# Graph-attention kernel: first block's attention applied to relu(LN(x)) before the product with W0, with a new order on every engine

## What is computed

```python
def _L0_gnn_ref(h, adj, W, a):                      # first block
    Wh = jnp.einsum('bnf,fo->bno', h, W)
    e_src = Wh @ a1;  e_dst = Wh @ a2               # a1, a2: halves of a
    e = e_src[:, :, None] + e_dst[:, None, :]
    e = jnp.where(e > 0, e, 0.2 * e)
    e = jnp.where(adj > 0, e, NEG_INF)
    attention = jax.nn.softmax(e, axis=2)
    kth = jax.lax.top_k(attention, 16)[0][:, :, -1:]
    attention = jnp.where(attention < kth, 0.0, attention)
    return jax.nn.elu(jnp.einsum('bij,bjo->bio', attention, Wh))
def _L1_gnn_ref(x, adj, ...):                       # second block
    for l in range(3):
        # scores from x @ attn_w[l], masked softmax, agg = attn @ x
        h = layernorm(x + agg, g1[l], beta1[l])
        ff = gelu(h @ W1[l] + b1[l]) @ W2[l] + b2[l]
        x = layernorm(h + ff, g2[l], beta2[l])
h = jnp.maximum(_layernorm(x), 0.0);  x = x + _L0_gnn_ref(h, adj, W, a)
h = jnp.maximum(_layernorm(x), 0.0);  x = x + _L1_gnn_ref(h, adj, ...)
```

## Time and profile before

| | |
|---|---|
| median of 3 runs | 2964.74 us |
| the profiled execution's own time | 2969.18 us |
| its span, first to last instruction | 2967.5 us |
| TensorE matmul busy | 2822.2 us (95%) |
| ScalarE busy | 2460.3 us (83%) |
| GpSimd busy | 2229.7 us (75%) |
| VectorE busy | 2056.3 us (69%) |
| DMA engines, mean share | 12% in the middle of the run |

### The profile page before, as it was taken

How to read it: one execution, slowest core, us unless ns; L and a number is a source line. 1 busy time by engine, 2 the same in 40 slices (tenths; PEclk the granted TensorE clock), 3 DMA queues, 4 the chain that set the end, 5 groups by cost and what they waited for, 6 DMA issues and landing times.

```text
span 2967.5 us, 59504 instructions
## 1 busy us (share of the span) xinstructions
PE 2822.2 (95%) x17632; PEld 2510.8 (85%) x17632; DVE 2056.3 (69%) x7275; ACT 2460.3 (83%) x4887; POOL 2229.7 (75%) x2410
## 2 busy tenths in 40 slices
PE   4789999999999999999999999999999999999985
PEld 3678888888888888888889888888888888988874
DVE  4667777767777676867777777776777767776432
ACT  3578899888898888889988888988888888888763
POOL 0356878878787788777878877777878778888874
PEclk6789999999999999999999999999999999999997
DMA  5100010111101111111011110011110101110001
GB/s 154 36 26 26 26 33 17 34 26 32 34 26 21 30 33 25 33 28 32 18 33 25 33 33 27 17 33 34 24 34 26 34 17 33 24 33 19 10 10 15
DMA packets 96388, 89.38 MB, mean 30 GB/s; under 512 B 9120, under 2 KB 94368, under 8 KB 96032
## 3 DMA queue, kind: packets, MB, share of 16 engines
q1 hardware_dynamic: 79136, 68.32, 7.6%
q0 software_dynamic: 16896, 16.78, 4.3%
HBM read 47.34 MB, written 37.75 MB: 29 GB/s over the span
## 4 chain that ended last, share of the span: by engine, by line
PE 54%; POOL 13%; issue 11%; DVE 11%; DMA 2%; ACT 1%; POOLq 0%; DVEq 0%; ACTq 0%
PE ps_ff L1114 7%; PE ps_ff L1115 7%; PE ps_ff L1116 7%; PE ps_mm L1093 7%; PE ps_mm L1094 7%; PE ps_mm L1095 7%; POOL a_lo L417 3%; PE ps_ag L1151 3%; PE ps L1204 2%; DVE junk L930 2%; PE ps_ht L1165 2%; POOL H L424 2%; DMA out<-H 2%; POOL H L407 2%; POOL H L396 2%
## 5 line engine op out<-in xcount | busy, mean ns | idle before, releaser
L417 POOL TENSOR_TENSOR a_lo<-A,a_hi 128x512 fp32r<-128x512 f32 x576 | 759.9, 1330 | 433.6 <-ACT a_hi L540 423.0
L1114 PE MATMUL ps_ff<-w_hi,a_hi 128*128 128x256 f32 x3072 | 902.3, 294 | 19.3 <-issue 10.4
L1115 PE MATMUL ps_ff<-w_lo,a_hi 128*128 128x256 f32 x3072 | 864.9, 282 | 1.0 <-issue 0.7
L1116 PE MATMUL ps_ff<-w_hi,a_lo 128*128 128x256 f32 x3072 | 859.6, 280 | 0.0
L532 ACT ACTIVATE A<-ps_mm,b_col 128x512 f32<-128x512 f32 x768 | 524.2, 685 | 226.8 <-PE ps_ff L1116 138.8
L1093 PE MATMUL ps_mm<-ht_hi,w_hi 128*128 128x512 f32 x1536 | 655.0, 426 | 3.6 <-DVE ht_lo L981 2.8
L1114 PEld LDWEIGHTS ps_ff<-w_hi,a_hi 128*128 128x128 f32 x3072 | 578.2, 188 | 50.6 <-issue 30.5
L1094 PE MATMUL ps_mm<-ht_hi,w_lo 128*128 128x512 f32 x1536 | 608.0, 396 | 0.0
L1095 PE MATMUL ps_mm<-ht_lo,w_hi 128*128 128x512 f32 x1536 | 607.1, 395 | 0.0
L1115 PEld LDWEIGHTS ps_ff<-w_lo,a_hi 128*128 128x128 f32 x3072 | 578.9, 188 | 18.6 <-issue 3.9
L1116 PEld LDWEIGHTS ps_ff<-w_hi,a_lo 128*128 128x128 f32 x3072 | 579.2, 189 | 0.0
(11 more groups left out here) (111 smaller groups left out, 5186.5 us busy)
## 6 DMA issues: line engine op xcount, KB each, us to landing
xr<-in_x SPq DMA_DIRECT2D x32, 512.0 KB, 3.8
out<-x SPq DMA_DIRECT2D x32, 512.0 KB, 3.5
out<-H POOLq DMA_DIRECT2D x32, 512.0 KB, 6.0
mask_in<-mask_park SPq DMA_DIRECT2D x96, 128.0 KB, 3.0
adj_sb<-in_adj SPq DMA_DIRECT2D x32, 256.0 KB, 4.4
mask_park<-mask_out SPq DMA_DIRECT2D x32, 128.0 KB, 1.7
X<-in_L_gnn_W SPq DMA_DIRECT2D x3, 1024.0 KB, 5.1
H<-in_L_gnn_W SPq DMA_DIRECT2D x3, 1024.0 KB, 7.7
```

Source lines behind the costliest of these rows:

```text
L417: pool.tensor_tensor(a_lo[:, at], A[:, at], a_hi[:, at].bitcast(F32), ALU.subtract).then_inc(s["a_lo_gpsimd"], 1)
L1114: pe.matmul(out_g, a_hi[:, at, cols], w2_hi[:, l, m], start=first, stop=False, skip_group_check=True)
L1115: pe.matmul(out_g, a_hi[:, at, cols], w2_lo[:, l, m], start=False, stop=False, skip_group_check=True)
L1116: last = pe.matmul(out_g, a_lo[:, at, cols], w2_hi[:, l, m], start=False, stop=final, skip_group_check=True)
```

## The change

First block: `x0_norm` applies relu itself. The score vectors come from relu(LN(x)) in SBUF and the vectors W0 a1 and W0 a2, made once (`wa_sums`, `turn_wa`, `wa_copy`). `z_mix` applies the attention to relu(LN(x)), `mix_copy` brings that product to SBUF, and `z_agg` multiplies it with W0. `turn_h0`, `h0_copy`, `wh`, `wh_copy` and `wh_scores` are gone. The split of the eight low parts (two on VectorE, six on GpSimd) is as before. All five orders are new, the iteration begins at another place of the work, and the hardware loop has 22 iterations (4 to 25) in 11 trips; 18 are unrolled.

```diff
-FIRST, LAST = -4, NG + 3
-FIRST_STEADY, LAST_STEADY = 4, NG - 5
+FIRST, LAST = -5, NG + 3
+FIRST_STEADY, LAST_STEADY = 4, NG - 7
...
-                norm("x", k, lambda g: hn0[:, g], lambda g: xr[:, g], ACT.Identity, s["x_norm"])
+                norm("x", k, lambda g: hn0[:, g], lambda g: xr[:, g], ACT.Relu, s["x_norm"])
...
+            def mix_copy(k, half):
...
+                act.wait_ge(s["z_mixed"], value(n + 1))
                 if some(n):
+                    act.wait_ge(s["z_agg"], value(n))
+                act.activation(flat(mixed[:]), ps_0[:], ACT.Copy).then_inc(s["mix_copied"], 1)
...
+            def wa_sums():
+                dve.wait_ge(s["w0_in"], 16)
+                dve.wait_ge(s["a0_in"], 16)
+                for j in range(2):
+                    for c in range(DC):
+                        last = dve.tensor_tensor_reduce(
+                            out=junk[:, 2 * j + c], in0=w0[:, c], in1=a0_row[:, j], scale=1.0, scalar=0.0,
+                            op0=ALU.mult, op1=ALU.add, accum_out=wa_col[:, j, c:c + 1])
...
+            def e0_scores(k):
...
+                dve.wait_ge(s["x_norm"], value(k + 1))
...
+                for g in range(G):
                     for j in range(2):
                         last = dve.tensor_tensor_reduce(
+                            out=junk[:, 2 * g + j], in0=hn0[:, g], in1=wa_row[:, j], scale=1.0, scalar=0.0,
+                            op0=ALU.mult, op1=ALU.add, accum_out=e0[:, j, g:g + 1])
...
             def turn_e0(k):
-                pe.wait_ge(s["wh_copied"], value(k * 2 + 2))
+                pe.wait_ge(s["e0_made"], value(k + 1))
                 pe.wait_ge(s["mask_made"], value(k * 2 + 1))
+                if some(k):
+                    pe.wait_ge(s["z_out_made"], value(k * 2))
...
+            def z_mix(k, half):
...
+                pe.wait_ge(s["pt0_made"], value(k + 1))
+                if some(n):
+                    pe.wait_ge(s["z_out_made"], value(n))
+                for c in range(DC):
+                    for g in range(2):
+                        j = 2 * half + g
+                        last = pe.matmul(ps_0[:, (2 * c + g) * P:(2 * c + g + 1) * P], hn0[:, j, c * P:(c + 1) * P], pt0[:, j * P:(j + 1) * P],
+                                         start=(c == 0 and g == 0), stop=(c == DC - 1 and g == 1), skip_group_check=True)
...
             def z_agg(k, half):
-                pe.wait_ge(s["pt0_made"], value(k + 1))
...
-                    last = pe.matmul(ps_0[:, g * D:(g + 1) * D], pt0[:, j * P:(j + 1) * P], wh_sb[:, j],
-                                     start=(g == 0), stop=(g == 1), skip_group_check=True)
+                pe.wait_ge(s["mix_copied"], value(k * 2 + half + 1))
                 for g in range(2):
+                    for c in range(DC):
+                        last = pe.matmul(ps_0[:, g * D:(g + 1) * D], mixed[:, c, g * P:(g + 1) * P], w0[:, c],
+                                         start=(g == 0 and c == 0), stop=(g == 1 and c == DC - 1), skip_group_check=True)
...
+                masks(i + 2)
                 a_low(i, 0, 7)
-                masks(i + 2)
...
```

More of the change, by code:

```diff
@@ L452, in iteration @@
             def iteration(i):
[L453 to L479, removed]
@@ L1166, in turn_h @@
                 last.then_inc(s["h_turned"], 1)
-            def turn_h0(k, half):
-                if not here(k):
-                    return
-                n = k * 2 + half
-                pe.wait_ge(s["x_norm"], value(k + 1))
-                if some(n):
-                    pe.wait_ge(s["wh_copied"], value(n))
-                if some(k):
-                    pe.wait_ge(s["z_out_made"], value(k * 2))
-                for d in range(DC):
-                    for g in range(2):
-                        last = pe.transpose(ps_0[:, (2 * d + g) * P:(2 * d + g + 1) * P],
-                                            hn0[:, 2 * half + g, d * P:(d + 1) * P], ident[:])
-                last.then_inc(s["h0_turned"], 1)
             def w1_bias(l):
@@ L1192, in w1_bias, with turn_wa @@
                 last.then_inc(s["w1_biased"], 1)
[L1194 to L1206 removed]
+            def turn_wa():
+                pe.wait_ge(s["wa_summed"], 1)
+                for j in range(2):
+                    for c in range(DC):
+                        last = pe.transpose(ps_0[:, j * D + c * P:j * D + (c + 1) * P], wa_col[:, j, c:c + 1].to_broadcast([P, P]), ident[:])
+                last.then_inc(s["wa_turned"], 1)
             def turn_e0(k):
@@ L1247, in iteration @@
-                mm1(i - 1, 1, 3)
-                turn_p(i + 1, 0)
-                turn_h0(i + 2, 1)
-                mm1(i - 1, 1, 4)
-                agg(i + 1, 0, 0)
-                wh(i + 2, 1)
-                mm2(i - 1, 1, 0)
-                mm2(i - 1, 1, 1)
-                agg(i + 1, 0, 1)
-                turn_h(i - 2, 2, 0)
+                turn_h(i - 2, 2, 1)
+                turn_e0(i + 2)
                 mm2(i - 1, 1, 2)
                 mm1(i - 1, 1, 5)
-                turn_e0(i + 2)
+                agg(i + 1, 0, 1)
@@ L1271, in iteration @@
-                mm2(i - 1, 1, 7)
+                mm1(i - 2, 2, 2)
+                mm1(i - 2, 2, 3)
                 if peeled(i, -1):
                     w1_bias(2)
-                mm1(i - 2, 2, 2)
-                mm1(i - 2, 2, 3)
-                turn_h(i + 1, 0, 0)
                 mm2(i - 2, 2, 0)
-                turn_sj(i, 1)
                 mm1(i - 2, 2, 4)
```

413 lines of the change are left out of this document (214 added, 199 removed).

## The result

| | before | after |
|---|---|---|
| median of the runs, us | 2964.49 (2963.42 to 2964.8) | 2911.3 (2908.08 to 2913.98) |
| ratio | | 0.982, 95% interval 0.980 to 0.984 |
| profiled execution, us | 2969.2, span 2967.5 | 2913.98, span 2912.3 |

The changed kernel is faster by 53 us, the forecast was 28. The time lies in the range, between the forecast (2937) and rival B (2905). The views of the trace of after are read in the order of the prediction.

What follows compares the result with a forecast made beforehand. TensorE bounds the kernel: 85.7 us of work in an unrolled iteration of 85.92. Less work 27, waits in the loop 3, unrolled iterations minus 2, start and end zero: 28 off 2964.7 gives 2937 us, range 2904 to 2962, chance 0.55.

Steps and rivals of the forecast that it cites:

- rival B: The new order leaves only TensorE's wait at its branch, 32 us more gained: 2905 us, chance 0.14.
- TensorE's work: Removed and added matmuls and transposes: 6.04 us a group becomes 5.20, a gain of 0.85, 27 us in all.
- ScalarE: Two copies and two table loads fewer an iteration; the copy between `z_mix` and `z_agg` is covered; nothing counted.
- Place (a): `node_scores` of layer 0 no longer stands behind VectorE's branch, so the 1.33 us lost at `turn_sj` each trip goes.
- Place (c): `a_low` of chunk 7, now behind `y1_sum`, `y1_moments` and `masks`: about 1.3 us of VectorE's branch comes through once a trip.
- Place (b): First `mm2` of layer 0, waiting for `y_sum`: 0.5 to 0.6 us an iteration left as is, bounds 0 and 1.
- The sum of waits: About 4 us a trip in 11 trips, 44 against 47: a gain of 3; unrolled iterations a loss of 2.
- Start and end: Earlier first reductions against `x_moments` waiting for W0 and a: zero, between a gain of 8 and a loss of 8 us.
- C: Rival: VectorE's dense stretch ahead of layer 0's `y_sum` adds 0.5 us in some 30 iterations: 2952 us, chance 0.12.
- D: Rival, no change: a ring through ScalarE and VectorE sets the period, TensorE reaches the same waits earlier: about 2963, chance 0.06.
- E: Rival: masks slowed by GpSimd ahead of `a_low` of chunk 7, 1.9 us more in 31 iterations: 2996 us, chance 0.10.
- F: Rival of a dearer `z_mix`, outside the range of 2904 to 2962 us; size not in the text; chance 0.03.

Runs made afterwards that it cites:

- unshift_after: The changed kernel with `wa_col`, a tile of 16 bytes, moved to the end of the allocation, so tiles between stand where they stood before: 2952.0 us, ratio 0.995.
- pad64_before: The kernel before with an unused tile of 64 bytes a partition behind `a0_row`: 2971.9 us, ratio 1.002.
- pad64_after: The changed kernel with an unused tile of 64 bytes behind `wa_col`: 2956.7 us, ratio 0.997 to the kernel before.
- all_by_64: The changed kernel with an unused tile of 64 bytes ahead of `w1_hi`, so every tile moves by 64 bytes: 2909.2 us, ratio 0.982 to the kernel before.
- pad16_before: The kernel before with an unused tile of 16 bytes behind `a0_row`, moving all tiles behind it by 32 bytes: 2954.8 us, ratio 0.996.
- trips_8: The changed kernel with 8 trips of the hardware loop for 11 and six more iterations written out: 2901.1 us, ratio 0.979 to the kernel before.
- masks_behind: The changed kernel with `masks(i + 2)` on VectorE behind `a_low` of chunk 7 instead of ahead of it: 2912.4 us.
- topk_earlier: The changed kernel with `z_recip` and `z_topk` ahead of `y_moments(i - 1, 1)` on VectorE: 3023.1 us, ratio 1.021 to the kernel before.

## Why the prediction was right, and where it was not

It was right that the kernel gets faster, and its range held the time. That the gain is not half of the forecast is luck: without the shift of the tiles, which the forecast did not have, it is half (2952.0 us, still in the range). The 53 us are two gains, and the forecast knew one of them: **14 us by the change's work and order (28 forecast) and 39 by the layout (0 forecast).** Point by point, with the kernel without the shift (`unshift_after`) for the first and the changed kernel for the second.

*TensorE's work: right.* The forecast has 0.85 us a group. Without the shift an unrolled iteration takes 85.03 us where it took 85.87 (mean of two). A `z_mix` record costs 0.112, inside the bounds of 0.108 to 0.128 (in the stretch of before that gave the upper one, 88.9 to 93.1 us, weight loads are busy for 4.08 of 4.20 us at a clock of 0.86; a half takes 0.9 to 1.0 with the longer first distance, 0.87 forecast). Doubling the products agrees: 16 records more lengthen an unrolled iteration by 1.7 us.

*ScalarE: right.* Its table loads fell from 302 to 244. `x0_norm` takes 590 ns with relu and took 596 without. TensorE waits nowhere in the loop for the copy ahead of `z_agg`. The forecast had some 0.5 us for the two hand-overs around that copy; where ScalarE waits for `z_mix`, the copy starts 0.31 to 0.46 us after the last record's start, and a weight load that waits for the copy starts 0.05 us after its end.

*Place (a): right.* The wait for `sij` is gone from the loop. *Place (c): right*, 1.4 us a trip where 1.3 was forecast, and by the named chain. *Place (b): wrong, to the good side.* The wait for `y_sum`, kept at about 0.5 an iteration, is gone; that was its bound of 0.

*The sum of waits: wrong.* "A trip keeps about 4 us of waits": without the shift it keeps 5.0. The step that failed is the list of three places. I looked where steps had been ahead of a wait before, and not at `turn_z`, which in the new order comes due before VectorE has done `z_topk`. TensorE's waits in the run without the shift, 1200 to 2400 us:

```profile
PE ps L1210 <- DVE U L893: 13.2, 13, 1.7
PE ps_ff L1120 <- DVE a_lo L995: 7.1, 6, 1.4
PE ps_ff L1120 <- issue: 4.8, 6, 1.0
```

Two waits at `turn_z`, 0.5 and 1.7 idle (0.6 and 1.8 from start to start), took the place of `sij` and `y_sum`. So 11 trips x 5.0 = 55 against 47, a loss of 8 where I had a gain of 3. The loss of 2 in the unrolled iterations did not come.

*Start and end: off by a sign that the bounds allowed.* The 49th first-kind `mm1` matmul (`w_hi` with `ht_hi`) starts at 229.8 before and at 236.5 without the shift; the 385th at 837.3 and 843.2. The start costs 6 us, against my zero within 8. 27 - 8 - 6 = 13; the spans differ by 12.6.

*The layout: not thought of.* The sum took the pitch of `mm1` and `mm2` from before as a property of the matmul: 85.7 us of work, 67.5 of it in these two terms. In these runs it is a property of the matmul and of where its operands stand. The term that was missing is 288 x 3.3 + 144 x 3.1 = 1.4 us a group by the means. An unrolled iteration fell by only 0.88: the distances inside `mm2` and `mm1` sum to 1.15 less, and 0.27 came back between the steps, which is not resolved further. A trip fell by 3.0 (175.0 to 172.0): twice 0.88, and 0.9 because the longer of the two waits at `turn_z` fell from 1.8 to 0.9.

*The rivals.* B named the right size for the wrong reason: the waits did not go. C and D fell. D, "TensorE reaches the same waits earlier", is not what the change did, but it is what the layout does in the kernel before, where 36 us of cheaper matmuls gave 12. E asked for the masks beside wide GpSimd operations; they took 1.56 us in the loop, near the quiet 1.48 of the start, beside GpSimd's operations of four columns, so it did not come about. F, a dearer `z_mix`, fell: a record costs 0.112 us.

## What to carry to other kernels

A change of a tile's size or of the order of allocations moves every tile behind it, and a kernel bound by TensorE can win or lose over 1% by that alone (39 of 2965 us here). Before an edit is credited with a gain, compare the distance between successive matmuls that it does not touch, and run it once with the old places restored. With a new order, list the waits that can appear as well as those that go. Where a wait stands next to a loop's branch, the branch can take back most of what is won there, as it did here (0.75 us a trip became 2.0). And where a reordering makes TensorE idle for longer, look at the granted clock behind the idle time: in the worst run here it was a third of the loss (some 35 of 112 us).

## What the runs showed of the hardware

- The distance in SBUF between a matmul's stationary and moving operand, modulo 128 bytes, changed its pitch in these runs. With 64, an fp32r matmul with 256 columns took 115.0 ns and one with 512 columns 229.8 (`after`); with 32, 118.3 and 232.9 (`before`); with 96, 118.5 and 233.4 (`pad64_before`); with 0, 119.1 and 231.9 (`pad64_after`). Moving both operands by 64 bytes changed nothing (`all_by_64`, 115.0 and 229.8). With the same 64, in the order of before, it was 115.7 and 230.3 (`pad16_before`). The loss against 64 was 2 to 4 ns for either width, and not in proportion to the columns; why is open, and distances that are no multiple of 32 were not tried. The other engines were at work in every run; the place of TensorE's own operands was enough to change the pitch, with the same work on the others (`unshift_after` against `after`: 3.3 and 3.2 ns). No run tried other types.
- A record of an fp32 matmul of 128 columns cost 0.112 us (`z_mix` in `after`), and one of a transpose in fp32 of the same width 0.109 (`turn_h0` in `before`).
- A hardware loop's trip cost 3.4 to 3.8 us in this kernel (`trips_8`: 10 us for 3 trips; `after`: 172.05 against two iterations of 84.1). TensorE's idle time at its own branch was 0.75 us with the wait for `a_low` ahead of it (`after`) and 2.0 us without (`masks_behind`).
- The granted clock fell from 1.00 to 0.50 for 3.4 us (once for 6.8), within 2 us of the end of idle times of TensorE of 2.3 to 2.95 us, 22 times in `topk_earlier` and 3 times in `masks_behind`, and never between 240 and 2780 us in the changed kernel or in `unshift_after`, whose waits there reach 1.5 and 1.7 us. A fall cost about 1.6 to 2 us.
